# A graph attention layer: the projection stage makes K alone, and Q, V and skip are made block by block in the score stage

## What is computed

```python
for l in range(L):                       # L = 2
    q = (x @ Wq[l] + bq[l]).reshape(N, H, D)
    k = (x @ Wk[l] + bk[l]).reshape(N, H, D)
    v = (x @ Wv[l] + bv[l]).reshape(N, H, D)
    a = (q[dst] * k[src]).sum(-1) * scale
    e = jnp.exp(a - amax[dst])           # amax: segment max of a over dst
    alpha = e / (denom[dst] + 1e-16)     # denom: segment sum of e
    agg = segment_sum(alpha[:, :, None] * v[src], dst).reshape(N, C)
    x = agg + (x @ Ws[l] + bs[l]) + enc
x = layer_norm(x, ln_g, ln_b)
x = relu(x @ W1 + b1) @ W2 + b2 + x      # then layer norms, residuals
```

## Time and profile before

| | us |
|---|---|
| median of three runs | 2437.12 (2436.15 to 2437.2) |
| the profiled execution | 2427.93 |
| its span, first to last instruction | 2426.2 |

### The profile page before, as it was taken

The page is one execution under the profiler, slowest core; times in us unless marked ns, Lnnn a source line. Parts: engine busy times, 40 slices in busy tenths (PEclk is TensorE's granted clock), DMA queues, the critical chain, the costliest instruction groups (busy, mean ns, idle before and its releaser), DMA issues. The chain is left out here.

```text
span 2426.2 us, 47903 instructions
## 1 busy us (share of the span) xinstructions
PE 1935.8 (80%) x8220; PEld 1313.4 (54%) x8221; DVE 1813.3 (75%) x2465; ACT 1457.2 (60%) x8263; POOL 1677.3 (69%) x1660
## 2 busy tenths in 40 slices
PE   2987888888389888877969888886498888859997
PEld 2873444444167555555844444442385555547876
DVE  5526878788798777775748777888897777778994
ACT  1325878787487666662238777787596666643222
POOL 2667777777667777764767777776677777747663
PEclk8997999999789999998989999999699999989999
DMA  2558989998667777766769999997677777761201
GB/s 91 209 194 315 300 300 297 300 301 284 184 191 210 209 211 209 210 196 227 262 253 300 299 300 300 301 300 217 186 210 211 210 210 210 210 214 53 70 35 50
DMA packets 188287, 536.02 MB, mean 221 GB/s; under 512 B 36132, under 2 KB 36516, under 8 KB 188136
## 3 DMA queue, kind: packets, MB, share of 16 engines
q0 software_dynamic: 116512, 381.77, 51.8%
q1 hardware_dynamic: 62984, 137.09, 16.0%
q10 hardware_dynamic: 8640, 15.73, 2.0%
HBM read 465.99 MB, written 68.17 MB: 220 GB/s over the span
## 5 line engine op out<-in xcount | busy, mean ns | idle before, releaser
L663 POOL DMA_INDIRECT score_rows<-k_rows,score_index x704 | 679.2, 965 | 216.2 <-issue 187.8
L663 POOL DMA_INDIRECT coll_rows<-v_rows,coll_index x704 | 667.9, 949 | 226.5 <-issue 205.4
L1030 PE MATMUL coll_banks<-coll_ev,coll_hot 128*128 128x260 f32 x2816 | 689.9, 393 | 131.4 <-DVE all_work L1102 112.4
L902 ACT ACTIVATE all_work<-all_work 128x64 f32<-128x64 f32 x2752 | 660.2, 241 | 196.9 <-DVE all_work L825 165.2
L1030 PEld LDWEIGHTS coll_banks<-coll_ev,coll_hot 128*128 128x128 f32 x2816 | 515.5, 190 | 305.7 <-DVE all_work L1102 231.8
L1165 ACT ACTIVATE coll_ev<-coll_rows,graph_edge 128x64 f32<-128x64 f32 x2112 | 542.5, 335 | 229.5 <-DMA coll_rows<-v_rows,coll_index 229.3
L782 PE MATMUL score_q_ps<-layer_q,all_work 128*128 x2112 | 530.6, 388 | 165.8 <-DVE all_work L825 138.8
L825 DVE TENSOR_TENSOR all_work<-score_q_ps,score_rows 128x1024 f32<-128x1024 f32 x352 | 429.0, 1219 | 160.9 <-DMA score_rows<-k_rows,score_index 118.5
L902 ACT ACTIVATION_READ_ACCUMULATOR all_work<-all_work (+1 forms) x2752 | 513.7, 187 | 0.0
L782 PEld LDWEIGHTS score_q_ps<-layer_q,all_work 128*128 128x128 bf16 x2112 | 192.7, 99 | 450.7 <-issue 301.3
L1090 DVE TENSOR_TENSOR coll_ev<-coll_rows,coll_banks 128x640 f32<-128x640 f32 x352 | 287.9, 818 | 135.0 <-DMA coll_rows<-v_rows,coll_index 131.0
(11 more groups left out here) (220 smaller groups left out, 2366.3 us busy)
## 6 DMA issues: line engine op xcount, KB each, us to landing
all_work<-local_dst SPq DMA_DIRECT2D x44, 512.0 KB, 7.9
x_turned<-proj_xt SPq DMA_DIRECT2D x40, 512.0 KB, 2.7
score_xt<-x_turned SPq DMA_DIRECT2D x40, 512.0 KB, 6.3
score_rows<-k_rows,score_index POOLq DMA_INDIRECT x704, 4.9
coll_rows<-v_rows,coll_index POOLq DMA_INDIRECT x704, 3.7
skip_rows<-proj_base POOLq DMA_DIRECT2D x40, 256.0 KB, 3.2
k_rows<-proj_k_out SPq DMA_DIRECT2D x40, 256.0 KB, 2.0
all_work<-skip_rows SPq DMA_DIRECT2D x40, 256.0 KB, 6.3
```

Of the source, the lines that this page charges most:

```text
L663: nc.gpsimd.indirect_dma_start(rows[:, slot, t, :], None, table, at).then_inc(arrived[slot], 16)
L902: last = nc.scalar.activation(at, at, ACT.Copy, accum_out=k.edge[:, bass.ds(n * TPS + t, 1), h:h + 1].rearrange("p a b -> p (a b)"))
L1030: last = nc.tensor.matmul(sums[s % SUMS][:, part, :], m, ev[:, s % EVS, t, part * AGG // 2:(part + 1) * AGG // 2], start=t == 0, stop=t == ...
```

## The change

- `project` becomes `keys`. It makes K alone, 12 matmuls a block. SP does all of its loads and stores, in one list. In layer 0 it also splits all eight weight matrices of both layers (ACT the high part, DVE the low part, from block 8 on one for each two blocks) and POOL writes the parts of six of them to DRAM (`k.w_d`); later stages load them from there. The transposes of the segment keys stand between the first blocks' products, and the flags of segment starts go to DRAM and come back in `soften_collect`.
- The blocks are ordered by falling count of their steps (`order_row`, `place_row`); SP reads a block's number from the table ahead of each block transfer.
- In `score`, PE makes Q, V and skip of one block per half, 3 x 13 matmuls, up to five a step. The bias is a thirteenth matmul with two rows (its high and low part) against ones. Q of the place that the next half needs is ready at its sixth step (Q_BY). ACT copies Q's high part (`q_hi`, after step 3) and V (`take_v`, after step 6), DVE makes Q's low part (`q_low`, step 4). Q is kept as two fp32r parts; the one-hot is fp32r, built by pairs of steps (four a half, in two buffers), from destinations loaded pair by pair (128 KB each). DVE sums three heads, ACT five. `prod` is two deep; rows and index stand in `k.work`. The skip base is the input itself.
- `score` ends with a clearing of its semaphores and a barrier (`give_back`).

```diff
-PRODS = 4
+PRODS = 2
-Q_PARTS = 3
-DVE_HEADS1, DVE_HEADS2 = 4, 5
+DVE_HEADS1, DVE_HEADS2 = 3, 5
+OUTS = 3
+SIDE = 3 * KC + 1
+PER_STEP = -(-OUTS * SIDE // HALF)
@@ build_step_tables: blocks in falling order of their steps
+                link(v.scalar_tensor_tensor(rank[:], n_steps[:], float(P), numbers, ALU.mult, ALU.subtract))
+                link(v.tensor_tensor(before[:], rank[:].unsqueeze(1).to_broadcast([P, BLOCKS, BLOCKS]),
+                                     rank[:].unsqueeze(2).to_broadcast([P, BLOCKS, BLOCKS]), ALU.is_gt))
+                link(v.tensor_tensor(steps_before[:], before[:], n_steps[:].unsqueeze(1).to_broadcast([P, BLOCKS, BLOCKS]),
+                                     ALU.mult))
+                link(v.tensor_reduce(steps_start[:], steps_before[:], AX.X, ALU.add))
+                link(v.tensor_tensor(steps_end[:], steps_start[:], n_steps[:], ALU.add))
...
@@ project -> keys
-def project(nc, k, layer):
+def keys(nc, k, layer):
...
+            matrices = [(l, n, m[l]) for l in range(LAYERS) for n, m in enumerate((k.Wk, k.Wq, k.Wv, k.Ws))]
+            split_at = [w_k, k.wq] + [split[i % 2] for i in range(2, len(matrices))]
...
+                def load(b):
+                    u = b % 2
+                    if first:
+                        if b >= 2:
+                            sp.wait_ge(turned, b - 1)
+                        sp.dma_start(x[:, u, :], k.x[b * P:(b + 1) * P, :]).then_inc(x_in[u], 16)
+                    else:
+                        if b >= 2:
+                            sp.wait_ge(x_ready, b - 1)
+                        sp.dma_start(skip[:, u, :], k.skip_d[layer - 1][b * P:(b + 1) * P, :]).then_inc(x_in[u], 16)
...
+                for b in range(BLOCKS):
+                    u = b % 2
+                    if b + 2 < BLOCKS:
+                        load(b + 2)
...
+                    sp.wait_ge(lo_ready, b + 1)
+                    sp.dma_start(k.xt_d[b * P:(b + 1) * P, :], xt[:, u].rearrange("p a c n -> p (a c n)").bitcast(F32)
+                                 ).then_inc(xt_stored[u], 16)
+                    sp.wait_ge(out_done, b + 1)
+                    sp.dma_start(k.k_d[b * P:(b + 1) * P, :], k_out[:, u, :]).then_inc(k_stored[u], 16)
...
+                    n = len(matrices)
+                    def load(i):
+                        if i >= 2:
+                            pool.wait_ge(w_lo, i - 1)
+                        pool.dma_start(raw[:, i % 2], matrices[i][2].rearrange("(c p) n -> p c n", p=P)).then_inc(raw_in[i % 2], 16)
+                    def store_split(i):
+                        l, which, _ = matrices[i]
+                        pool.wait_ge(w_lo, i + 1)
+                        for part in range(2):
+                            pool.dma_start(k.w_d[l, which, part], flat_w(split_at[i][part]).bitcast(F32)).then_inc(split_out[i % 2], 16)
...
+                for b in range(2, BLOCKS):
+                    high_part(b)
+                    if first and b - 2 < QUARTS:
+                        copy_keys(b - 2)
+                    elif first and b % 2 == 0 and b // 2 - 2 < len(matrices):
+                        weight_high(b // 2 - 2)
...
+                for b in range(BLOCKS):
+                    if b + 1 < BLOCKS:
+                        low_part(b + 1)
+                    if not first and b + 2 < BLOCKS:
+                        assemble(b + 2)
+                    take_keys(b)
...
@@ side_product
+    if c == KC:
+        return nc.tensor.matmul(out, ones, bias, start=False, stop=True)
+    a, b = ((0, 0), (0, 1), (1, 0))[n]
+    return nc.tensor.matmul(out, xt[:, a, c, :], w[b][:, c, :], start=c == 0 and n == 0, stop=False)
@@ score
-        prod = in_work(PRODS * TPS * C).rearrange("p (r t n) -> p r t n", t=TPS, n=C)
+        rows = in_work(RING * TPS * C).rearrange("p (r t n) -> p r t n", t=TPS, n=C)
+        prod = in_work(PRODS * TPS * C).rearrange("p (r t n) -> p r t n", t=TPS, n=C)
+        index = in_work(2 * HALF * TPS).bitcast(I32).rearrange("p (q n) -> p q n", q=2)
+        q = ph.sb("q", [P, BLOCKS * 2 * C], F32R)
+        hot = ph.sb("hot", [P, 2, PAIR], F32R)
+        local = ph.sb("local", [P, 2, PAIR], BF16)
...
+                def locals_of(half, slots):
+                    for i in slots:
+                        sp.wait_ge(hot_ready, PAIRS * half + i + 1)
+                        load_local(PAIRS * half + i + 2, i % 2)
+                def run_half(half, q, skip_before, place, next_place, now_base):
+                    locals_of(half, (0,))
+                    if skip_before is not None:
+                        store_skip(half, skip_before)
+                    locals_of(half, (1,))
+                    if now_base:
+                        node = first_node(place)
+                        sp.wait_ge(skip_stored, 16 * half)
+                        load_base(node)
+                    if next_place is not None:
+                        node = first_node(next_place)
+                        sp.wait_ge(skip_product, half)
+                        load_xt(node, q)
+                    locals_of(half, (2, 3))
+                    if place is not None:
+                        node = first_node(place)
+                        sp.wait_ge(v_done, half + 2)
+                        sp.dma_start(k.v_d[bass.ds(node, P), :], v_out[:]).then_inc(v_stored, 16)
+                load_xt(first_node(0), 0)
...
-                                for part in range(Q_PARTS):
-                                    last = nc.tensor.matmul(q_ps[s % 2][:, t, :], hot[:, q, e:e + P],
-                                                            q3[:, part * C:(part + 1) * C],
-                                                            start=part == 0, stop=part == Q_PARTS - 1)
+                                for part in range(2):
+                                    last = nc.tensor.matmul(q_ps[s % 2][:, t, :], hot[:, s // HOT_STEPS % 2, e:e + P],
+                                                            parts[:, part * C:(part + 1) * C], start=part == 0, stop=part == 1)
+                            for i in range(s * PER_STEP, (s + 1) * PER_STEP):
+                                if i < len(items):
+                                    if i == 0:
+                                        pe.wait_ge(xt_in[u], 16 * (it + h + 1))
+                                    product(items[i], u, half)
...
-                            if s == HALF // 2 and (with_blocks or q == 0):
-                                one_hot(HALF * half + HALF, 1 - q, it + q + 1)
-                            if with_blocks and s == HALF - 2:
-                                take_v(half)
-                        if with_blocks:
-                            take_skip(half, q, it)
+                            if s % HOT_STEPS == 0 and not (ends and s == HALF - HOT_STEPS):
+                                ahead = s // HOT_STEPS + 1
+                                one_hot(PAIRS * half + ahead, ahead % 2, PAIRS // 2 * half + ahead // 2 + 1)
+                            if s == 1 and sides[h][0]:
+                                take_skip(half)
+                            if s == 4 and sides[h][1]:
+                                q_low(half + 1)
...
+                        if s % HALF == 3 and sides[s // HALF][0]:
+                            q_hi(half + 1)
+                        if s % HALF == 6 and sides[s // HALF][1]:
+                            take_v(half)
...
+        ph.give_back()
```

761 lines of the change are left out of this document (394 added, 367 removed).

## The result

| | before | after |
|---|---|---|
| median | 2436.64 us | 2491.6 us |
| span of the profiled execution | 2426.2 us | 2494.6 us |
| first gather of K, layer 0 | 184.4 | 190.5 |
| from there to the first gather of V (score stage, layer 0) | 454.9 | 502.9 |
| from there to the next first gather of K (collect, then keys of layer 1) | 605.5 | 573.4 |

The change made the kernel **slower: ratio 1.0219, 95% interval 1.0201 to 1.0237**. The forecast was 2414 us, the range 2385 to 2452: both missed. The stretch with the keys stage of layer 1 gave 32 us; the two score stages took 90.

A forecast was written before the change was run, and what follows sets the result against it. POOL's gathers were taken to bound the score stage, PE the projection stage. Terms +1 - 4 - 37 + 2 x (6 + 2.5) = -23 us took the median from 2437.1 to 2414 us, range 2385 to 2452.

The forecast's parts named there:

- Bound before, POOL's gathers: Score stage before the change: POOL sets the pace, 352 gathers at 1.25 us each need 440 us.
- Tables, +1: Tables: about 1 us more of small DVE operations for the order by size.
- Keys stage of layer 1, -37 us: Layer-1 keys stage: half the matmuls go, K outputs 4.8 us apart, first gather at 1208 in place of 1244.7.
- Keys stage of layer 0, -4 us: Layer-0 keys stage: 43 MB with weight splits, first gather at 180 against 184.4; from -14 to +8.
- Score stage, +8.5 a layer with its barrier: Score stage: +6 a layer (0 to +12), and +2.5 a layer for semaphore clearing and barrier at its end.
- the term for ACT, 20.3 us a half: Score stage: 80 sums take ACT 19.1 us a half, with two copies 20.3, level with POOL.
- Two product buffers in place of four hold DVE to two steps ahead of ACT: Score stage: fewer product buffers limit DVE's lead over ACT to two steps; no size given.
- Rival 1: Score stage: SP becomes the bound, destinations land late; with 2 us later landings +40, 2454 us; chance 0.18.
- +6.6 a layer: Score stage: four shorter one-hots a half hold gathers 0.5 us in place of 0.2, over 22 halves.
- Rival 2: Layer-1 skip loads hidden, layer-0 DMA at 395 GB/s, score stage +3: 2380 to 2398 us; chance 0.15.
- Rival 3 (every one-hot holds the gathers): Score stage: gathers held for each one-hot's full length, 1.5 us a half, 2467 us; chance 0.04.
- Rival 4: Layer-0 keys stage: block and weight stores share DMA, rates fall to 280 GB/s, +22, 2436 us; chance 0.13.

The follow-up runs named there:

- version with four heads: Changed kernel with four heads' sums on DVE, skip rows in layer 1 asked for earlier, weight splits from block 4: 2424.37 us, ratio 0.9960.
- run with the new order: Changed kernel, layer-1 keys stage asks for block b+3's skip rows ahead of the wait for block b's K output: 3139 us, ratio 1.0154, chip with DMA stops.
- early splits: Six later weight matrices split from block 4, not block 8, in layer 0; run with four DVE heads and earlier layer-1 skip loads: 2424.37 us, ratio 0.9960.
- the base: The changed kernel as it is, measured again, on a chip without DMA stops: 2489.28 us, ratio 1.0228.
- run with the copies on DVE: Changed kernel, three heads on DVE, with Q's high part and V's output copied by DVE in place of ACT: 2488.81 us, ratio 1.0229.
- four buffers: Changed kernel with four product buffers in place of two, low part of skip weights left out: ratios 1.0374, 1.0422 and 1.0386, chips with DMA stops.
- four destination buffers: Changed kernel with four destination buffers, not two, low skip weights left out: 1.0193, 1.0217, 1.0166; with four DVE heads too 1.0002; chips with DMA stops.
- the third piece ahead: Third destinations piece asked for before the skip-store wait: with four DVE heads, earlier skip loads and weight splits 0.9957; on the changed kernel alone 1.0132.

## Why the prediction was wrong

*Bound before, POOL's gathers: right.* The version with four heads comes near that bound again, 20.7 us a half against 20.0, with POOL waiting 23 us of 390 for DVE.

*Tables, +1: right* (the stage behind them starts at 43.8 and not 42.1).

*Keys stage of layer 1, -37 us: right.* It gave 148.4 - 116.4 = 32. The first K output came 18 us into the stage, as reckoned (1113 - 1095), and the next seventeen 4.6 to 6.2 us apart, 5.1 in the mean where 4.8 was reckoned, with DVE's add waiting for the skip load:

```profile
1218.27 0.69 DVE L603 TENSOR_TENSOR keys_x<-keys_x,keys_skip 128x512 f32<-128x512 f32 x1 [1.22 <-DMA keys_skip<-skip_rows]
1218.88 0.68 DVE L585 TENSOR_TENSOR keys_k_out<-keys_out_ps,keys_bias_k 128x512 f32<-128x512 f32 x1
1223.02 0.69 DVE L603 TENSOR_TENSOR keys_x<-keys_x,keys_skip 128x512 f32<-128x512 f32 x1 [0.95 <-DMA keys_skip<-skip_rows]
1223.63 0.68 DVE L585 TENSOR_TENSOR keys_k_out<-keys_out_ps,keys_bias_k 128x512 f32<-128x512 f32 x1
```

The run with the new order confirms the chain: it took the waits away, and the outputs came 4.2 us apart in the mean, most of them 3.8 (1181.15, 1184.99, 1188.84 in the run with four heads), where 3.5 was reckoned for DVE.

*Keys stage of layer 0, -4 us: wrong by 8.* The stage took 146.6 us for 142.3 from its start to the first gather. The bytes were right (298 GB/s x 146.6 = 43.7 MB for 43) and so was the end of the blocks (176 reckoned, last K output 177.9). The step that failed is the last, "the first gather 4 us later": the split of the eighth matrix stands in block 18, so 2 MB are still to be written when the blocks are through, and POOL has to see them land.

```profile
177.81 0.53 POOL L457 DMA_DIRECT2D weights<-keys_split_lo  x1
189.13 0.19 POOL L686 COPY all_work<-graph_src_t 128x16 int32<-128x16 int32 x1 [10.78 <-POOLq L95]
190.45 1.03 POOL L699 DMA_INDIRECT all_work<-k_rows,all_work  x1 [1.13 <-issue]
```

From the last K output to the first gather 12.6 us, where the sum had 4. The early splits confirm it and show why they gained so little. There the last weights were asked for at 161.3 and the time from the last K output to the first gather fell to 5.3 us, in both kernels that have them (it is 11.4 to 13.2 in all the changed kernels with late splits, and was 11.3 in the kernel before, where the trace could have told it). But the last K output itself came later, at 182.3 and 183.9 in place of 175.0 to 180.9: the bytes of the weights had only moved from behind the blocks to beside them.

```profile
186.24 0.19 POOL L688 COPY all_work<-graph_src_t 128x16 int32<-128x16 int32 x1 [24.40 <-POOLq L95]
```

The bounds given for this term hold an arithmetic slip: 30 MB at 325 GB/s are 92 us, which gives +4 and not +8.

*Score stage, +8.5 a layer with its barrier: it was +48.0 and +42.5, and this is the miss.* The terms: PE's 2.0 us a step hid, as said. ACT's work of 20.3 us a half was right as far as it went: 352.3 of 390 us is 19.9 for a half of 22.0 in the base. **What failed is the term for ACT, 20.3 us a half and so level with POOL.** The sum left out the stop at the turn of ACT's loop, 3.8 us once in sixteen steps: 30.6 of 390 us, 1.7 a half, and 19.9 + 1.7 = 21.6 of the 22.0 measured. It was in the trace of before, as the 19.8 us of "issue" above. The seventeen sums of the earlier trace rows were chosen without a gap and couldn't show it. By the trace alone, then, ACT is the new bound of the stage from its fourth half on, and the run with four heads shows how much hangs on it: 29 and 24 us of the miss go, 24.4 of them in layer 0 in the eighteen halves that were timed and 4.9 in the first three. What the stop by itself costs no run shows, since none takes it away and leaves the sums.

"Two product buffers in place of four hold DVE to two steps ahead of ACT" was written down and given no price. Two steps are about 5 us of lead, and a stop of 3 to 5 us eats most of it; then DVE, PE's next product and POOL's ring wait as well, as the rows at 483.77 to 488.20 show. That the lead costs time beside ACT's load is likely by the run with the copies on DVE, where ACT waited 22.9 us for DVE and DVE 52.6 for ACT in the same 390 us; it is not shown, since the one direct test, four buffers, was slower, on chips where ACT's issue waits are three to four times as long.

(The path over ACT was also added up wrong, which changes little: 18.5 + 20 x 20.3 + 16 x 2.2 is 460 and not 457.)

About 18 us a stage are left with four heads, by layer 0. From the multiplies (201.72, 268.11, 640.05) the first comes 4.0 us sooner after the first gather than before, and the first three halves take 66.4 us for 53.9, 12.5 more. That is a start-up price which the sum bounded only by its first multiply ("no later than 18.5 us", which held: 14.6). The waits that the trace shows on DVE there are for destinations (6.3 us), for PE (6.0) and for issue (4.3). The other 18 halves take 20.66 each, +11.3; the waits for destinations beside them (38 us of 390, 2.0 a half) would be enough, but no run shows it.

*Small terms.* DVE 15.8 to 17 us a half: 286 of 390 is 16.2. The one-hot, 0.43 to 0.68: 0.48. The one-hots hold the gathers for less and not for more than before, so the +6.6 a layer reckoned for that was not there: from 240 to 630 us 23 of 277 gathers are over 0.97 us, by 1.8 us in all, where 16 of 308 were, by 4.2. Nothing in the balance calls for more than the 2.5 us a layer for the barrier.

*Rival 1 (SP late, slower, 0.18)* ended on the right side, and its mechanism is in the trace, but it isn't the main cause: 26.7 us of DVE's waits against 62.5 for ACT, and one more head on DVE takes most of the miss with the waits for destinations left, even longer (38.1 in place of 23.7 us of 390). It is the next in line once ACT is relieved. What it costs there stays open: the runs with four destination buffers and with the third piece ahead all ran on chips where the one-hot waited for no destinations. *Rival 2* fell with the skip loads not hidden. *Rival 3 (every one-hot holds the gathers)*: no. A gather took 953 ns in the mean, less than the 965 before; the median is 946 in both.

```profile
L663 POOL DMA_INDIRECT score_rows<-k_rows,score_index x704 | 679.2, 965 | 216.2 <-issue 187.8
L699 POOL DMA_INDIRECT all_work<-k_rows,all_work x704 | 670.7, 953 | 298.6 <-issue 176.7
```

The rule of the Trainium skill that was weighed there ("SBUF — State Buffer", section "SBUF: two separate sides") came closest to the measured time, by a mechanism that the trace doesn't show. *Rival 4* (layer 0, +26 over the forecast) was right in sign, at a third of its size.

*The signs* named ahead showed it at once: "if ACT's sums stall on the two product buffers" is DVE's 62.5 us of waits for ACT, "if the layer-0 stage is longer than 141 us" came true too (146.6), and "ACT with hardly any idle time" stood in the forecast itself. An engine reckoned to be level with the bound, with its lead halved, should have been the slower rival with the largest chance.

## What to carry to other kernels

When a change brings a second engine level with the one that sets the pace, add up everything that this engine does in a turn of its loop, the stop at the turn among it, from a stretch that holds a whole turn and not from a run without gaps. Compare the lead that the buffers between two engines give with the longest stop of either (here two steps, about 5 us, with stops of 3 to 5); if they are cut in the same change that loads an engine, price both together, and plan a run that parts them. A deeper buffer didn't help the overloaded engine here: look what else stands in its queue, here Q's high part, for which PE waits. And look whether the wait that a run is to remove stands in a trace of the same kind of chip: two of the edits here were tried where it didn't.
